# Differential attention with a mixture of experts: the value products of a step in one block of 512 queries at its end

## The reference, cut to what matters

```python
Q1, Q2 = jnp.split(Q, 2, axis=-1)          # 16 heads, two halves of 16 features
K1, K2 = jnp.split(K, 2, axis=-1)
A1 = jnp.einsum('bhqd,bhkd->bhqk', Q1, K1) * scaling
A2 = jnp.einsum('bhqd,bhkd->bhqk', Q2, K2) * scaling
attn = jax.nn.softmax(A1, axis=-1) - lamb * jax.nn.softmax(A2, axis=-1)
out = jnp.einsum('bhqk,bhkd->bhqd', attn, V)
```

## Time and profile before

| | |
|---|---|
| median of 3 runs | 3233.37 us (3232.21 to 3233.64) |
| profiled execution, its span | 3232.2 us |
| PE busy | 3089.3 us, 96% |
| DVE busy | 2735.8 us, 85% |
| ACT busy | 2502.6 us, 77% |
| POOL busy | 453.2 us, 14% |
| mean granted TensorE clock | 0.982 |

### The profile page before, as it was taken

How to read it: one execution, slowest core, us unless ns; L and a number is a source line. 1 busy time by engine, 2 the same in 40 slices (tenths; PEclk the granted TensorE clock), 3 DMA queues, 4 the chain that set the end, 5 groups by cost and what they waited for, 6 DMA issues and landing times. The chain is left out here.

```text
span 3232.2 us, 72457 instructions
## 1 busy us (share of the span) xinstructions
PE 3089.3 (96%) x29281; PEld 1389.4 (43%) x29282; DVE 2735.8 (85%) x2902; ACT 2502.6 (77%) x4689; POOL 453.2 (14%) x654
## 2 busy tenths in 40 slices
PE   8999999999999999999999999999999969999995
PEld 4333333333333333333333333333332658999995
DVE  3599999999999999999999999999998683433443
ACT  3269999999999999999999999999999552333333
POOL 2000000000000000000000000000000464555554
PEclk9989999999999999999999999999999979999997
DMA  6520101111020101011010101021002561222224
GB/s 159 124 45 15 35 21 30 30 34 28 15 35 24 28 15 35 29 30 28 28 28 18 34 21 28 15 51 28 15 9 83 206 227 34 38 38 36 36 37 124
DMA packets 101213, 152.92 MB, mean 47 GB/s; under 512 B 21592, under 2 KB 64464, under 8 KB 99248
## 3 DMA queue, kind: packets, MB, share of 16 engines
q1 hardware_dynamic: 85008, 130.03, 16.2%
q0 software_dynamic: 15904, 18.66, 3.6%
HBM read 88.35 MB, written 60.29 MB: 46 GB/s over the span
## 5 line engine op out<-in xcount | busy, mean ns | idle before, releaser
L1005 DVE TENSOR_REDUCE half_max<-scores 128x2 f32<-128x1024 f32 x2016 | 2297.4, 1219 | 10.5 <-PE scores L759 4.8
L930 ACT ACTIVATE probs<-bank 128x512 f32<-128x512 f32 x4012 | 2142.3, 595 | 142.5 <-PE bank L772 45.5
L831 PE MATMUL bank<-probs,V 128*32 128x256 f32 x16384 | 1309.6, 391 | 44.2 <-ACT probs L930 42.4
L759 PE MATMUL scores<-K,Q 48*128 48x512 f16 x4032 | 793.9, 388 | 3.0 <-SPq L542 2.2
L772 PE MATMUL bank<-Q,K 50*128 50x512 f16 x4012 | 789.7, 380 | 0.0
L831 PEld LDWEIGHTS bank<-probs,V 128*32 128x32 f32 x16384 | 322.5, 108 | 583.2 <-issue 517.7
L759 PEld LDWEIGHTS scores<-K,Q 48*128 48x128 f16 x4032 | 194.2, 93 | 834.6 <-DVE half_max L1005 532.2
L772 PEld LDWEIGHTS bank<-Q,K 50*128 50x128 f16 x4012 | 371.2, 94 | 183.0 <-ACT probs L930 4.2
L660 POOL TENSOR_SCALAR max_parts<-row_max 128x16 f16<-128x16 f32 x64 | 16.2, 253 | 2066.3 <-DVE row_max L1011 2066.3
L1604 ACT ACTIVATE h<-u 128x1024 f32<-128x1024 f32 x71 | 75.0, 1057 | 260.8 <-DVE u L1648 260.8
L1565 PE MATMUL pre<-xgT,w 128*128 128x128 f32 x2272 | 265.3, 275 | 2.3 <-ACT xgT L1598 2.3
(11 more groups left out here) (195 smaller groups left out, 1204.8 us busy)
## 6 DMA issues: line engine op xcount, KB each, us to landing
attended<-att SPq DMA_DIRECT2D x64, 256.0 KB, 2.5
W<-in_L_ffn_w_dram SPq DMA_DIRECT2D x16, 1024.0 KB, 6.4
Q<-q_parts SPq DMA_DIRECT2D x96, 128.0 KB, 6.6
K<-k_parts SPq DMA_DIRECT2D x96, 128.0 KB, 6.9
values<-attended SPq DMA_DIRECT2D x6, 2048.0 KB, 9.2
q_parts<-parts SPq DMA_DIRECT2D x64, 128.0 KB, 2.4
k_parts<-parts SPq DMA_DIRECT2D x64, 128.0 KB, 2.4
xT<-in_x_cols_dram SPq DMA_DIRECT2D x8, 512.0 KB, 4.9
```

What stands on the lines that cost most here:

```text
L759: mm = nc.tensor.matmul(scores[:, b, h, :], Q[p][r, c, up, t * P:(t + 1) * P], K[p][r, up, kc * TC:(kc + 1) * TC], start=True, stop=True)
L831: mm = nc.tensor.matmul(banks[att_bank[s // KB]][32 * u:32 * u + 32, q], V[wp][:, wk, u // 2, :], probs[:, 4 * s % RING + u, q], start=(wk ...
L930: nc.scalar.activation(probs[:, i % RING, :], banks[tile_bank[i]][:], ACT.Exp, scale=SCALE).then_inc(exp_done, 1)
L1005: nc.vector.tensor_reduce(half_max[lc % 2][:, :, up, t, kc], scores[:, b], AX.X, ALU.max).then_inc(max_done[b], 1)
```

## The change

`weigh` loses its argument `part`: it takes all 512 queries at once, so that a step has four float32 matmuls of 512 queries in place of eight of 256. It is called once, behind the second score pair and the second two transposed tiles. Its waits are the same and stand at its head.

```diff
-                        def weigh(s, part):
+                        def weigh(s):
                             wp, wk = s // KB // CH, s % KB
-                            if part == 0:
-                                if wk == 0:
-                                    pe.wait_ge(exp_done, it * 4 * RS + att_after[s // KB] + 1)
-                                else:
-                                    pe.wait_ge(exp_done, it * 4 * RS + 4 * s + 4)
-                                if s % (CH * KB) == 0:
-                                    pe.wait_ge(v_copied, 2 * it + wp + 1)
+                            if wk == 0:
+                                pe.wait_ge(exp_done, it * 4 * RS + att_after[s // KB] + 1)
+                            else:
+                                pe.wait_ge(exp_done, it * 4 * RS + 4 * s + 4)
+                            if s % (CH * KB) == 0:
+                                pe.wait_ge(v_copied, 2 * it + wp + 1)
                             for u in range(UNITS):
-                                q = slice(TC // 2 * part, TC // 2 * (part + 1))
-                                mm = nc.tensor.matmul(banks[att_bank[s // KB]][32 * u:32 * u + 32, q], V[wp][:, wk, u // 2, :],
-                                                      probs[:, 4 * s % RING + u, q],
-                                                      start=(wk == 0 and part == 0), stop=(wk == KB - 1), skip_group_check=True)
-                            if part == 1:
-                                mm.then_inc(pv_done, 1)
+                                mm = nc.tensor.matmul(banks[att_bank[s // KB]][32 * u:32 * u + 32, :], V[wp][:, wk, u // 2, :],
+                                                      probs[:, 4 * s % RING + u, :],
+                                                      start=(wk == 0), stop=(wk == KB - 1), skip_group_check=True)
+                            mm.then_inc(pv_done, 1)
...
-                        weigh(j, 0)
                         if item < STEPS:
                             score_pair(item, ahead // KB, ahead % KB * 2)
                         transposed(it, j, lc, 0)
-                        weigh(j, 1)
                         if item < STEPS:
                             score_pair(item, ahead // KB, ahead % KB * 2 + 1)
                         transposed(it, j, lc, 1)
+                        weigh(j)
```

## The result

| | before | after |
|---|---|---|
| median | 3232.8 us (4 runs) | 3615.8 us (4 runs, 3611.3 to 3619.5) |
| span of the profiled execution | 3232.2 us | 3611.1 us |
| mean granted TensorE clock (1.00 is full speed in the profile's count) | 0.982 | 0.985 |

The ratio is 1.118 (95% interval 1.117 to 1.120). The prediction said 3614 us.

A forecast was written before the change was run, and what follows sets the result against it. VectorE was taken to pace the loop at 2.28 us a step, TensorE 0.04 short of it. The new step, 1.13 + 0.32 + 1.00 + 0.22 = 2.67 us, over 1001 steps gave 3614 us; 80% range 3560 to 3690.

The forecast's parts named there:

- run 381: Not a run label: forecast growth of the whole run, +379.1 us in the loop, +2 for half-clock first steps.
- The fixed path of 1.13 us: From T0 to a step's fourth tile, which awaits the first tile's exponential to free its bank: 0.48 + 0.60 + 0.05 us.
- The block at 1.00 us: The merged value products of 512 queries take 1.00 us per step; lower end 0.96, upper end 1.14.
- The merge saves 0.14 us of TensorE work: Value products: a real saving of 0.14 us, but from work that no longer sets the time.
- The change between tilings: On TensorE, one change between tilings per step saved on top of the merge's 0.14 us; no size given.
- T0: Queue entry of a step: its first two transposed score tiles, 4s and 4s+1.
- S1: Queue entry of a step: its second maxima score pair.
- the first rival: Fourth tile's wait doesn't bind, VectorE stays the bound: 3223 us, or no difference; chance 0.03 faster, 0.03 no difference.
- VectorE idle by about 390 us: Sign of being right: VectorE's maxima in the main loop idle by about 1001 x (2.67 - 2.28) = 390 us.
- Boundaries at nothing: At chunk boundaries the 0.68 us product wait goes but brings no gain: put at 0, at most 6 us.
- S0: Queue entry of a step: its first maxima score pair, forecast 0.22 us ahead of T0.
- The clock: Rival: holes in TensorE's queue halve the granted clock, 4.21 us a step, 5154 us in all; chance 0.04.

The follow-up runs named there:

- short exponentials: Kernel before, with ScalarE taking exponentials of queries 0 to 255 of each tile only: 3218.4 us, ratio 0.995.
- the block in the middle: Changed kernel with the 512-query block between the first two transposed tiles and the second maxima score pair: 3579.8 us, ratio to before 1.108.
- the quarter: Kernel before with products split unevenly: 384 queries at the step's head, 128 between the first transposed tiles and second score pair: 3442.1 us, ratio 1.065.
- the older bank: Kernel before, with the attended sum taking the bank of the last tile but two at chunk boundaries: 3219.0 us, ratio 0.996.

## Why the prediction was right

The step was forecast at 1.13 + 0.32 + 1.00 + 0.22 = 2.67 us and is 2.667 as the median of the loop; the loop was to be 379 us longer, the whole run 381, and the span grew by 3611.1 - 3232.2 = 378.9. The mechanism held, term by term. That the total fits to a few us is partly luck: the rows are read to 0.01 us, which over 1001 steps is 10 us, and the four runs after the change lie 8 us apart. Point by point:

- *The fixed path of 1.13 us.* Right, and tested three ways: it stands unchanged with 128 queries inside it, it moves to the other pair when the block moves (1.07 there), and it shrinks one for one with the exponential. That the fourth tile waits on it already in the kernel before was in the two rows of its load, though the idle times don't show it; the run of before with short exponentials bears it out, with 0.02 us a step.
- *The block at 1.00 us.* Right, from the last step's back-to-back row; the two other full shapes would have given 0.96.
- *The merge saves 0.14 us of TensorE work.* Right in sum, but the term was laid to the wrong edit: the 16 unmerged matmuls together take 1.00 as well. The saving is in putting the halves next to each other; the merge itself is worth some 6 us in all. The change between tilings, which the prediction put on top, stands for 0.10 us of a step: T0 to S1 takes 0.22 (701.20 to 701.42), where T0 to the products took 0.32 before (701.04 to 701.36 in the earlier trace rows). That the tiling is what costs these 0.10 us is the author's guess; no run tested it apart. (The 2.0 us a step of TensorE in the first rival are 0.32 + 1.00 + 3 x 0.22 from the earlier trace rows, an estimate; the shortest median step that a run here shows is 2.22 us, in the kernel before with short exponentials.)
- *VectorE idle by about 390 us.* Mis-sized: its idle time rose from 10.5 to 300.5, by 290. Another 88 us are in its busy time (2385.1 against 2297.4 for all 2016 maxima before): a maximum that follows another counts 1.14 us, one that starts alone its full 1.22. The two together, 378, are the loop's growth.
- *Boundaries at nothing.* Right for this change: the products show no idle time before them. In the two experiments that moved or kept that wait (the block in the middle, the quarter), I carried the nothing over and was 36 and 38 us low.
- *What bounds the kernel before.* Half right. VectorE and TensorE are nearly level, but it is TensorE's order that sets the time. From the scores of one step to those of the next it takes 2.24 us in fifteen steps of sixteen, and 2.99 in the one with the boundary wait, as these rows of before show (S0 of the last step of a chunk and of the first two of the next):

```profile
1037.21 0.39 PE L759 MATMUL scores<-K,Q 48*128 48x512 f16 x2
...
1040.20 0.39 PE L759 MATMUL scores<-K,Q 48*128 48x512 f16 x2
...
1042.44 0.39 PE L759 MATMUL scores<-K,Q 48*128 48x512 f16 x2
```

A chunk is 15 x 2.24 + 2.99 = 36.59 us. With the older bank, where VectorE is busy throughout the window 300:2400, it takes 36.44 (16 times the mean step of 2.278). So VectorE's idle time before, 0.15 us a chunk, is TensorE's boundary wait arriving there, and its true limit is 14 to 15 us below, as the older bank and the short exponentials show. The prediction read the 0.04 us between 2.24 and 2.28 as room on TensorE's side; the boundary wait used it up.
- *The clock.* The rival didn't come: 1.00 in the window 300:2700, with TensorE busy 2125.2 of 2400 us (89%, as worked out beforehand). That idle times of 0.3 us, once a step, could bring the clock down, as this rival supposes, no run here shows.

The other rivals fall with the step: the wait binds in 1001 of 1001 steps, and the block didn't cost 1.14.

## What to carry to other kernels

Where an engine's queue is in order and a buffer ring ties a late item to an early one, work placed between the two hides the round trip; moving it all to one side as one block bares it, even if the block itself becomes cheaper. Here the products of a step fell from 2 x 0.57 to 1.00 us, and the step rose from 2.24 to 2.67. Look for such a tie in the start of the load or issue of the waiting instruction against the end of what releases it: in this case a gap of 0.05 us that came back in every order marked a wait, also where the idle time was nil. And an engine that is busy 99% doesn't make its neighbours free: here TensorE's order, with its wait at the chunk boundary, needed 0.15 us a chunk more than VectorE.

## What the runs showed of the hardware

The form of the product matmuls hardly matters: 16 float32 matmuls of 256 columns in four column groups, back to back, take the same 1.00 us as 8 of 512 (counted as the trace does, two for each float32 matmul). An exponential costs 0.597 us for 512 columns and 0.383 for 256, 0.214 for the difference; from 512 to 1024 columns (1.092 us, the median of the 42 that read `scores` in the kernel before, L937) it is 0.495. So no straight line runs through all three, and what an exponential would cost at very few columns isn't shown. An idle time of 0.31 us in each step of 2.67 us left the granted clock at 1.00 over the 2400 us of the window 300:2700.
